# State-space stage: skip products issued behind the exponential, the gated tile's high part in its own step, and the second tile's taps behind the gated tile

## Chip, cores and metric

The kernel runs on 1 core of one Trainium2 chip. The metric is the device time of one execution in microseconds (us), as the median of several executions. All activation and weight tensors are float32; products that must be exact to float32 are split into high and low parts of type fp32r, so that one product becomes three matmuls (high by high, high by low, low by high).

## The reference, cut to what matters

Four layers, each added to a residual after a layer norm: a selective state-space layer (Mamba-2 form), a ternary feed-forward layer, a causal attention and a mixture of 8 experts. The change lies in the first. For 2 sequences of 512 tokens, 64 heads of 64 channels in 8 groups, and a state of 128:

```
proj = hidden @ in_proj_w.T                # gate, x|B|C, dt
xBC  = silu(conv_bias + sum_k shift(hbc, k) * conv_weight[:, k])   # 4 taps
state = state * exp(dt*A) + dt*x (outer) B ;  y = state . C + D*x
var  = mean over the 512 channels of a group of y*y
yn   = y * rsqrt(var + eps) * norm_weight * silu(gate)
out  = yn @ out_proj_w.T
x    = x + layernorm(out)
```

## The kernel before, in words

The state-space stage works group by group (g = 0 to 7, 512 channels each: 4 tiles of 128 channels for x, one for B, one for C). Within a group it goes through steps s = 0 to 7, one for each piece of 128 tokens (4 pieces make one sequence; c is the piece's number in its sequence). `group_steps` writes the steps out for group 0, in a hardware loop for groups 1 to 6, and for group 7, which has two more steps (8 and 9) to drain. Each engine has its own `step` function; the order of the lines in it is the order in which that engine works, and semaphores tie the engines together. A step holds work on three token pieces at once, s, s-1 and s-2:

- TensorE (PE): transposes of piece s (L1604, L1608) and its B.C product (L1610), the decay exponents of piece s (L1618, called D here, into banks 2 and 3), the convolution input of a first new tile (L355 with wch and wcl, 12 passes, bank 0), the column sum of squares of piece s-2 (L1635), then for piece s-1 the product with the entering state (L1644, into bank 6, for c > 0), the products within the piece (L1650, into bank 7) and the state's addition (L1659, into bank 6, for c < 3), the convolution input of a second tile (L355, bank 2), a tile of the gate (L355 with wgh and wgl, bank 0), and last the output product of piece s-2 (L355 with ynTh, ynTl, woh and wol, 12 passes, bank 1).
- Steps 0, 1, 2, 4, 5, 6 have two convolution tiles each; steps 3 and 7 have none, nor have steps 3 to 9 of the last group. D writes bank 2, so it waits until VectorE has applied the taps to the second tile of the step before (`taps`).
- ScalarE (ACT): the copy of the transposed piece s to `xtok` (L965), the high part `ynTh` of piece s-2 (L969), the exponential of piece s in banks 2 and 3 (L974), the first tap and the tanh of each convolution tile (L927, L935), the sum's scaling `ssv` (L986), the square of y of piece s-1 (L993), the gate's tanh (L941), and last the four skip products `xd` = D*x of piece s (L1002). Besides: casts of the next group's weights, in step 2 (L955, woh), step 3 (L979, wch) and step 5 (L1014, wgh, ahead of the exponential), and the scaling of the next output weights at the end of step 7 (L1020).
- VectorE (DVE): copies and mask of piece s (L1291, L1294), the low part `ynTl` of piece s-2 (L360), the masked decays `em` of piece s (L1304), the entering part y (L1278), taps of the first tile (L1200, three instructions), y of piece s-1 (L1316, L1319, which needs `xd`), the state (L1325 or L1328), silu of the first tile (L1206), taps of the second tile (L1200), the gated tile yn of piece s-1 written to bank 6 (L1340), the gate's product (L1253), silu of the second tile (L1206), and the addition of the output of piece s-2 to `acc` (L1351). In the last group each addition is followed by a round of the next layer norm on the piece (`norm_round`: L612, L617, L623, L628, L633, L636).
- GpSimd (POOL): the two halves of the squares' sum (L726, L728), the decays `am` of piece s+1 (L710), low parts of weights (L360: wol in step 2, wcl in steps 3 and 4, wgl in step 5), the state's decay (L746), `dtx` and `xdec` of piece s (L756, L761) and the reciprocal root `rg` (L767).
- SyncE (SP) loads the next group's weights as their buffers come free and the decay factors of each piece (`grown_load`). The diff does not touch it.

Bank 6 holds in turn the product with the entering state, the state's addition and yn. PE's L1644 and L1650 in a step wait for `ynT_lo` of piece s-2, which says that bank 6 has been read; the output product waits for it too. `ynTh` may be overwritten only when the output product of the piece before is done (`o_ready`).

## Time and profile before

| what | us |
|---|---|
| median of 3 runs | 1781.15 |
| the 3 runs | 1765.92, 1786.74, 1781.15 |
| the profiled execution, its own time | 1772.24 |
| its span from first to last instruction | 1770.5 |
| state-space stage, groups 0 to 7 | from about 98 to 1048 |
| one group of the loop | about 117 |

The times in rows are us from the start of the span, durations in rows of groups "mean ns of one". Idle time stands in brackets with what ended it. PE is TensorE's matmuls, PEld its weight loads, which overlap them. A run of matmuls shows the first one's start and the last one's end.

### The profile page before, as it was taken

To read this page: it belongs to the slowest core of one execution; us is meant where nothing else is said; L and a number is where in the kernel's file an instruction comes from. 1 tells how busy PE (TensorE), PEld (TensorE's weight loads), DVE (VectorE), ACT (ScalarE), POOL (GpSimd) and SP (SyncE) were. 2 spreads that over 40 slices of the span, in tenths; PEclk is the share of its full clock that TensorE was granted. 3 is DMA by queue.
4 is the path that set the end of the run, shared out by engine and by line. 5 is a ranking of instruction groups with operands and counts; after the bars stand their busy time and mean duration, and the time that the engine had idled before them with its cause. 6 is when DMAs were issued, how large, how long until landed. Compare 5 with 4: busy or idle time off the path is not lost.

```text
span 1770.5 us, 26605 instructions
## 1 busy us (share of the span) xinstructions
PE 1561.6 (88%) x8870; PEld 1227.9 (69%) x8870; DVE 1221.4 (69%) x2024; ACT 827.5 (47%) x1639; POOL 942.9 (53%) x861
## 2 busy tenths in 40 slices
PE   3789999999999999999999759996789999987791
PEld 2567877877878778778787647885557776766581
DVE  5467778777787777787787665556657767768525
ACT  2355554554554545555554323332147666764131
POOL 3257667577576675775766744004544423328444
PEclk9899999999999999999999878998889999998796
DMA  3102111012021110110211012222000000041335
GB/s 115 36 4 81 34 46 61 16 47 62 14 86 27 47 54 17 47 62 12 77 39 43 18 60 72 71 78 77 0 1 13 13 1 1 1 167 72 119 132 166
DMA packets 49497, 92.60 MB, mean 52 GB/s; under 512 B 8016, under 2 KB 32720, under 8 KB 44176
## 3 DMA queue, kind: packets, MB, share of 16 engines
q1 hardware_dynamic: 45744, 79.58, 14.1%
q0 software_dynamic: 3680, 12.06, 2.1%
q8 instruction: 43, 0.70, 0.2%
q14 instruction: 30, 0.25, 0.0%
HBM read 81.14 MB, written 10.49 MB: 52 GB/s over the span
## 4 chain that ended last, share of the span: by engine, by line
PE 61%; DVE 16%; POOL 8%; issue 7%; ACT 4%; DMA 3%; SPq 1%; POOLq 0%; ACTq 0%; DVEq 0%
PE banks L355 31%; PE banks L1726 6%; PE banks L1852 3%; PE banks L1650 3%; PE banks L1644 3%; PE banks L1736 3%; PE banks L1817 2%; POOL wol L360 2%; DMA x<-in_w_gate 2%; DVE tap L1200 2%; PE banks L1842 2%; PE banks L1659 2%; PE banks L1618 2%; DVE acc L623 2%; DVE xbc L1206 1%
## 5 line engine op out<-in xcount | busy, mean ns | idle before, releaser
L1200 DVE SCALAR_TENSOR_TENSOR tap<-banks,parg,tap 128x511 f32<-128x511 f32 (+2 forms) x288 | 215.0, 747 | 41.4 <-ACT tap L927 33.9
L710 POOL TENSOR_TENSOR am<-ah,upto 128x1024 fp32r<-128x1024 f32 x64 | 126.4, 1975 | 214.0 <-PE banks L1618 198.9
L862 POOL TENSOR_SCALAR kz<-kst,head 128x512 fp32r<-128x512 f32 x64 | 99.1, 1568 | 159.9 <-DVE kst L1427 159.9
L355 PE MATMUL banks<-xTh,wch 128*128 128x512 f32 x384 | 163.4, 425 | 7.0 <-DVE em L1304 6.8
L355 PE MATMUL banks<-xTh,wcl 128*128 128x512 f32 x384 | 151.3, 394 | 0.0
L355 PE MATMUL banks<-xTl,wch 128*128 128x512 f32 x384 | 151.1, 394 | 0.0
L1132 ACT ACTIVATE prob<-banks,nmax 128x128 f32<-128x128 f32 (+3 forms) x256 | 121.8, 530 | 54.5 <-DVE nmax L1438 54.4
L935 ACT ACTIVATE th<-tap 128x512 f32<-128x512 f32 x96 | 60.4, 630 | 171.4 <-DVE tap L1200 169.2
L1438 DVE TENSOR_REDUCE nmax<-banks 128x2 f32<-128x256 f32 (+3 forms) x128 | 104.7, 818 | 40.3 <-PE banks L1843 40.2
L710 POOL TENSOR_TENSOR am<-al,upto 128x1024 fp32r<-128x1024 f32 x64 | 121.9, 1904 | 0.0
L927 ACT ACTIVATE tap<-banks,parg 128x512 f32<-128x512 f32 x96 | 74.5, 776 | 91.4 <-PE banks L355 90.4
L355 PE MATMUL banks<-xTh,wgh 128*128 128x512 f32 x256 | 107.9, 421 | 5.2 <-POOL wgl L360 4.7
L1304 DVE TENSOR_TENSOR em<-banks,gmask 128x1024 f32<-128x1024 f32 x64 | 78.2, 1222 | 43.1 <-ACT banks L974 42.7
L355 PE MATMUL banks<-woh,ynTh 128*128 128x512 f32 x256 | 103.5, 404 | 4.0 <-DVE ynTl L360 4.0
L1852 PE MATMUL banks<-ident,prob 128*128 128x128 f32 x640 | 95.6, 276 | 10.7 <-DVE pB L1448 7.2
L355 PE MATMUL banks<-xTh,wgl 128*128 128x512 f32 x256 | 101.7, 397 | 0.0
L355 PE MATMUL banks<-woh,ynTl 128*128 128x512 f32 x256 | 101.3, 396 | 0.0
L355 PE MATMUL banks<-xTl,wgh 128*128 128x512 f32 x256 | 101.1, 395 | 0.0
L355 PE MATMUL banks<-wol,ynTh 128*128 128x512 f32 x256 | 100.7, 393 | 0.0
L355 PEld LDWEIGHTS banks<-xTh,wch 128*128 128x128 f32 x384 | 72.8, 190 | 36.7 <-DVE em L1304 13.4
L1726 PE MATMUL banks<-xTh,gu 128*128 128x512 f32 x224 | 90.1, 402 | 2.8 <-ACT gu L1059 2.8
L1206 DVE SCALAR_TENSOR_TENSOR xbc<-th,tap 128x512 f32<-128x512 f32 x96 | 90.9, 947 | 0.8 <-ACT th L935 0.8
(289 smaller groups left out, 4396.7 us busy)
## 6 DMA issues: line engine op xcount, KB each, us to landing
x<-grownT SPq DMA_DIRECT2D x96, 128.0 KB, 4.7
x<-in_w_conv SPq DMA_DIRECT2D x7, 1536.0 KB, 6.5
x<-in_w_gate SPq DMA_DIRECT2D x8, 1024.0 KB, 5.0
x<-in_w_out SPq DMA_DIRECT2D x8, 1024.0 KB, 4.8
eraw<-in_expert_w SPq DMA_DIRECT2D x8, 1024.0 KB, 7.2
gur<-in_ff_gu SPq DMA_DIRECT2D x7, 1024.0 KB, 4.8
x<-in_hidden SPq DMA_DIRECT2D x16, 256.0 KB, 3.8
mates<-yd SPq DMA_DIRECT2D x8, 512.0 KB, 4.4
```

The source lines that it names most:

```text
L355: m = nc.tensor.matmul(o, a, b, start=first and n == 0, stop=last and n == len(terms) - 1)
L710: m = pool.tensor_tensor(am[:, part, :, :], a[:, i, :].bitcast(F32).unsqueeze(2).to_broadcast([P, HG, P]), upto[:, :].unsqueeze(1).to_broa ...
L862: m = pool.tensor_scalar(kz[:, quad % 2, p2, j, :], kst[:, p2, :].bitcast(F32), head[:, j:j + 1], None, ALU.mult)
L927: nc.scalar.activation(tap[:, q % 2, :], bk(CONV_BANKS[q % 2]), ACT.Identity, bias=parg[:, CT * KC + q:CT * KC + q + 1], scale=parg[:, KC ...
L935: nc.scalar.activation(th[:, :], tap[:, q % 2, :], ACT.Tanh).then_inc(tanh_ready, 1)
L1132: e = nc.scalar.activation(prob[:, n % 2, j, 0:kw], bk(2 * (n % 2) + j)[:, 0:kw], ACT.Exp, bias=nmax[:, n % 2, j:j + 1])
L1200: nc.vector.scalar_tensor_tensor(tap[:, q % 2, sh:L], bk(CONV_BANKS[q % 2])[:, 0:L - sh], parg[:, KC * q + k:KC * q + k + 1], tap[:, q % 2 ...
L1206: nc.vector.scalar_tensor_tensor(xbc[:, q, b * L:(b + 1) * L], th[:, :], 1.0, tap[:, q % 2, :], ALU.add, ALU.mult).then_inc(xbc_ready, 1)
L1304: nc.vector.tensor_tensor(em[:, s % 2, :, :], decayed, gmask[:, :].unsqueeze(1).to_broadcast([P, HG, P]), ALU.mult).then_inc(m_ready, 1)
L1438: nc.vector.tensor_reduce(nmax[:, n % 2, :], banks[:, 2 * (n % 2):2 * (n % 2) + 2, 0:kw], AX, ALU.max, negate=True).then_inc(max_ready, 1)
L1726: m = mat(bk(2 * w + ft), gu[:, k, ft, w, :], part[:, k, tok], start=(k == 0 and part is xTh), stop=(k == KT - 1 and part is xTl))
L1852: m = pe.transpose(bk(4 + j)[:, c * P:(c + 1) * P], prob[:, w % 2, j, c * P:(c + 1) * P], ident[:, :])
```

## The change

On ScalarE, `ynTh` is no longer made for piece s-2 near the head of step s but for piece s-1 as the last item of step s (ahead of the output weights' scaling in step 7); and the skip products are made for piece s-1 in step s, behind the exponential (and behind the weight casts of step 3), instead of for piece s at the end of step s. On VectorE, yn of piece s-1 is made directly behind the state, ahead of silu of the first tile and of the second tile's taps; `ynTl` of piece s-1 is made at the end of step s, ahead of the addition to `acc`, instead of `ynTl` of piece s-2 near the head; and the copy of the skip factors in step 0 goes to the end of that step, with a second count of `cur_ready` that ScalarE waits for in step 1. No instruction is added or taken away but that count; PE and SP keep their order, and GpSimd's differs by one semaphore value.

```diff
@@ pool, step
                 if s == 0:
-                    pool.wait_ge(cur_ready, g + 1)
+                    pool.wait_ge(cur_ready, 2 * g + 1)
@@ act, step
                     nc.scalar.copy(xtok[:, s % 2, :], bk(4)).then_inc(x_out, 1)
-                if not (first and s < 2):
-                    act.wait_ge(yn_ready, NT * g + i + 1)
-                    at_least(act, o_ready, NT * g + i)
-                    nc.scalar.copy(ynTh[:, :, :], kt(bk(6))).then_inc(ynT_hi, 1)
                 if s == 5 and not last:
                     gate_high(g + 1)
...
                         nc.scalar.copy(couple(wch, n), couple(conv_stage(1), n)).then_inc(wc_hi, 1)
+                if not (first and s == 0) and s <= NT:
+                    at_least(act, y_ready, NT * g + s - 1)
+                    if s == 1:
+                        act.wait_ge(cur_ready, 2 * g + 2)
+                    j = (s - 1) % NT
+                    for k in range(KT):
+                        n = nc.scalar.activation(xd[:, k, :], xbc[:, k, j * P:(j + 1) * P], ACT.Copy, scale=skipg[:, k:k + 1])
+                    n.then_inc(xd_ready, 1)
                 if tiles:
                     first_tap(n0 + tiles[0], tiles[0] % CT)
...
                 if tiles:
                     tanh(n0 + tiles[1], tiles[1] % CT)
-                if s < NT:
-                    if not (first and s == 0):
-                        act.wait_ge(y_ready, NT * g + s)
-                    for k in range(KT):
-                        n = nc.scalar.activation(xd[:, k, :], xbc[:, k, s * P:(s + 1) * P], ACT.Copy, scale=skipg[:, k:k + 1])
-                    n.then_inc(xd_ready, 1)
+                if not (first and s == 0) and s <= NT:
+                    act.wait_ge(yn_ready, NT * g + s)
+                    at_least(act, o_ready, NT * g + s - 1)
+                    nc.scalar.copy(ynTh[:, :, :], kt(bk(6))).then_inc(ynT_hi, 1)
@@ dve, step
-                if not (first and s < 2):
-
-                    dve.wait_ge(ynT_hi, NT * g + s - 1)
-                    low(nc.vector, ynTl[:, :, :], kt(bk(6)), ynTh[:, :, :]).then_inc(ynT_lo, 1)
...
-                if s == 0:
-                    nc.vector.tensor_copy(skipg[:, :], skip[:, bass.ds(g, 1), :].rearrange("p g k -> p (g k)"))
...
+                if making:
+                    dve.wait_ge(gate_used, NT * g + 4 + KT * (i // CH) if i >= 0 else NT * g)
+                    if c < CH - 1:
+                        dve.wait_ge(state_ready, m + c + 1)
+                    dve.wait_ge(sq_ready, NT * g + i + 1)
+                    nc.vector.tensor_tensor(kt(bk(6)), kt(bk(7)), gate_at(i % NT), ALU.mult).then_inc(yn_ready, 1)
                 if s == 3 and not last:
                     dve.wait_ge(wc_hi, 3 * g + KT + 1)
                     low(nc.vector, couple(wcl, 0), couple(conv_stage(1), 0), couple(wch, 0)).then_inc(wc_lo2, 1)
                 if tiles:
                     silu(n0 + tiles[0], tiles[0] % CT, tiles[0] // CT % NB)
                     convolve(n0 + tiles[1], tiles[1] % CT)
-                if making:
-                    dve.wait_ge(gate_used, NT * g + 4 + KT * (i // CH) if i >= 0 else NT * g)
-                    if c < CH - 1:
-                        dve.wait_ge(state_ready, m + c + 1)
-                    dve.wait_ge(sq_ready, NT * g + i + 1)
-                    nc.vector.tensor_tensor(kt(bk(6)), kt(bk(7)), gate_at(i % NT), ALU.mult).then_inc(yn_ready, 1)
                 if gate:
...
                 if tiles:
                     silu(n0 + tiles[1], tiles[1] % CT, tiles[1] // CT % NB)
+                if s == 0:
+                    nc.vector.tensor_copy(skipg[:, :], skip[:, bass.ds(g, 1), :].rearrange("p g k -> p (g k)")).then_inc(cur_ready, 1)
+                if making:
+
+                    dve.wait_ge(ynT_hi, NT * g + i + 1)
+                    low(nc.vector, ynTl[:, :, :], kt(bk(6)), ynTh[:, :, :]).then_inc(ynT_lo, 1)
                 i = s - 2
                 if not (first and s < 2):
                     dve.wait_ge(o_ready, NT * g + i + 1)
```

## Rows read from the trace of the kernel before

**Rows 1.** The page: busy time by engine.
```profile
PE 1561.6 (88%) x8870; PEld 1227.9 (69%) x8870; DVE 1221.4 (69%) x2024; ACT 827.5 (47%) x1639; POOL 942.9 (53%) x861
```

**Rows 2.** Windows: one loop group, the last group (busy us by engine, clock, DMA).
```profile
449.00:566.00 117.00, 113.72 (x630) 92.01 (x630) 91.48 (x137) 61.31 (x120) 79.94 (x69) 1.00 0.17 45
917.00:1046.00 129.00, 106.55 (x572) 85.00 (x571) 91.39 (x159) 49.27 (x102) 81.15 (x82) 0.91 0.14 42
```

**Rows 3.** Waits of PE, 98 to 1046: total us, times, longest.
```profile
PE banks L1644 <- DVE ynTl L360: 21.9, 20, 3.3
PE banks L1635 <- ACT xtok L965: 8.5, 8, 1.2
...
PE banks L355 <- DVE ynTl L360: 4.0, 1, 4.0
PE banks L1650 <- DVE ynTl L360: 3.6, 1, 3.6
```

**Rows 4.** Waits of PE in one loop group, 449 to 566.
```profile
PE banks L1644 <- DVE ynTl L360: 1.5, 2, 0.9
PE banks L1635 <- ACT xtok L965: 1.2, 1, 1.2
```

**Rows 5.** Timeline of PE, step 3 of that group: start, us, what, idle before.
```profile
492.12 1.20 PE L1618 MATMUL banks<-am,after 128*128 128x512 f32 x4
494.51 0.35 PE L1635 MATMUL banks<-ones,y 128*128 128x1 f32 x2 [1.19 <-ACT xtok L965]
...
495.80 1.16 PE L1644 MATMUL banks<-xbc,state 128*128 128x128 f32 x8 [0.93 <-DVE ynTl L360]
```

**Rows 6.** Timeline of ACT, end of step 2 and head of step 3.
```profile
492.63 1.26 ACT L1002 ACTIVATE xd<-xbc,skipg 128x128 f32<-128x128 f32 x4
493.80 0.56 ACT L965 COPY xtok<-banks 128x512 f32<-128x512 f32 x1
```

**Rows 7.** Timeline of DVE, steps 2 and 3 of that group.
```profile
487.28 0.69 DVE L1328 TENSOR_TENSOR state<-banks,state 128x512 f32<-128x512 f32 x1 [1.65 <-POOL state L746]
487.89 1.95 DVE L1206 SCALAR_TENSOR_TENSOR xbc<-th,tap 128x512 f32<-128x512 f32 x1
489.76 2.31 DVE L1200 SCALAR_TENSOR_TENSOR tap<-banks,parg,tap 128x511 f32<-128x511 f32 x3
...
495.06 0.68 DVE L360 TENSOR_TENSOR ynTl<-banks,ynTh 128x512 fp32r<-128x512 f32 x1
```

**Rows 8.** Instructions that touch th: ns min/median/max of the silu, over 96.
```profile
L1206 DVE SCALAR_TENSOR_TENSOR xbc<-th,tap x96: 679/684/4346, 60.7 to 965.5; 128x512 f32<-128x512 f32 x96
```

**Rows 9.** Timeline of DVE, step 0 (456) and step 5 (532): the second tile's taps.
```profile
456.37 2.31 DVE L1200 SCALAR_TENSOR_TENSOR tap<-banks,parg,tap 128x511 f32<-128x511 f32 x3
...
532.36 2.31 DVE L1200 SCALAR_TENSOR_TENSOR tap<-banks,parg,tap 128x511 f32<-128x511 f32 x3
```

**Rows 10.** Timeline of PE: D of steps 1 and 6, which wait for those taps.
```profile
461.26 1.18 PE L1618 MATMUL banks<-am,after 128*128 128x512 f32 x4
...
535.91 1.18 PE L1618 MATMUL banks<-am,after 128*128 128x512 f32 x4
```

**Rows 11.** Timeline of ACT, step 0: the square that the gated tile waits for.
```profile
455.96 0.59 ACT L993 ACTIVATE y<-banks 128x512 f32<-128x512 f32 x1
```

**Rows 12.** Window of 3.4 us behind step 3's waits, another group (clock third from last).
```profile
613.80:617.20 3.40, 3.40 (x19) 2.15 (x17) 3.13 (x4) 1.89 (x4) 3.19 (x5) 0.50 0.06 14
```

**Rows 13.** Timeline of DVE, last group, steps 8 and 9.
```profile
1027.27 0.75 DVE L1351 SCALAR_TENSOR_TENSOR acc<-banks,rg,acc 128x512 f32<-128x512 f32 x1 [0.21 <-PE banks L355]
...
1030.57 0.68 DVE L360 TENSOR_TENSOR ynTl<-banks,ynTh 128x512 fp32r<-128x512 f32 x1
...
1047.87 0.75 DVE L1351 SCALAR_TENSOR_TENSOR acc<-banks,rg,acc 128x512 f32<-128x512 f32 x1 [4.77 <-PE banks L355]
```

**Rows 14.** Timeline of PE, the same stretch.
```profile
1031.31 2.08 PE L1644 MATMUL banks<-xbc,state 128*128 128x128 f32 x8 [2.21 <-DVE ynTl L360]
...
1043.25 0.47 PE L355 MATMUL banks<-woh,ynTh 128*128 128x512 f32 x1 [4.05 <-DVE ynTl L360]
```

## The prediction

> **What bounds the kernel now.** I read the page's busy times first, then windows of one group each, then PE's waits in the stage that the diff touches, and last the timelines of the steps where those waits lie. PE is busy for 1561.6 of 1770.5 us and no other engine passes 69% [rows 1]. The reader is to see that this is an average: in a loop group PE works 113.72 of 117 us at full clock, in the last group 106.55 of 129 us at a mean clock of 0.91 [rows 2]. So a loop group offers 3.3 us of idle PE, seven such groups some 23 us; the last group offers over 20 us and a clock. Whatever the change does on ScalarE and VectorE counts only where PE waits for them.
>
> PE's waits name the change's subject: for `ynTl` it waits 21.9 us before L1644, 4.0 us before the last output product and 3.6 us before one L1650, 29.5 us together; for `xtok` 8.5 us in 8 places [rows 3]. One loop group has 1.5 us of the first (steps 3 and 7) and 1.2 us of the second (step 3) [rows 4]. Seven groups make 10.6 us for `ynTl`; the other 18.9 us lie in the last group, where no convolution stands between D and L1644 and the layer norm's instructions stand ahead of `ynTl` on DVE.
>
> **Step 3 of a loop group.** Before: D runs 492.12 to 493.32, then PE waits 1.19 us for `xtok` and 0.93 us for `ynTl` [rows 5]. `xtok` is late because the four skip products (1.26 us) stand ahead of it on ACT [rows 6]. After: `ynTh` of piece 1 takes their place, a copy of the same size as `xtok` (0.56 us). ACT is free for it at 492.63, the output product before it ended before 492, so `xtok` ends at 492.63 + 0.56 + 0.56 = 493.75 instead of 494.36, 0.6 us earlier. On DVE the second tile's taps end at 489.76 + 2.31 = 492.07 [rows 7]; then come the gate's product, silu and now `ynTl` at once, 3 x 0.68: done at 494.1 instead of 495.74. L1644 then starts at 494.2 instead of 495.80: 1.6 us. The copies and the mask now follow `ynTl` and the addition, so the entering part y starts about 495.5; before, it started 0.1 us behind L1644's end. Of the 1.6 us I therefore take 1.4 us. Bounds: 0.3 us, if those taps come later (below) and hold D; 2.1 us, both waits gone.
>
> The skip products of step 3 now stand behind the exponential and three casts (some 4 us) on ACT. They are needed at L1319, which DVE reached 5 us behind the exponential's start; by that they arrive level with it, between 0.5 us early and 0.7 us late. DVE then only reaches the next group's low part later, and PE is in the gate and output products by then (24 passes, 5.5 us), so I take 0; uncovered it would cost 0.7 us.
>
> **Step 7.** PE waits 0.6 us for `ynTl` (1.5 less 0.9 [rows 4]). `xtok` of step 7 gets `ynTh` ahead of it, which waits for the output product just ended: 0.2 us later; and y follows the mask instead of `ynTl`. I take 0.2 us, between 0 and 0.6. The scaling of the output weights (four instructions, some 2.6 us) now waits behind `ynTh`, which waits for the end of PE's step 7, so `xtok` of the next step 0 comes 1.6 us later; a convolution tile (12 passes, 2.8 us) lies on PE between D and the sum that needs it: 0 with 0.6 us to spare.
>
> **Steps 0, 1, 2, 4, 5, 6: what the order on DVE costs.** The gated tile needs the square, and ACT does that behind the second tile's first tap. Silu of the first tile and the second tile's taps used to fill that wait; now they stand behind it. Step 0: the square ends at 455.96 + 0.59 = 456.55 [rows 11]; then yn 0.69, silu 0.68 and taps 2.31 end at 460.3 instead of 456.37 + 2.31 = 458.68 [rows 9]. D starts at 461.26 [rows 10]: 0.9 us to spare, cost 0. Steps 1, 4 and 6 have the same order and nearly the same distance. In step 2 the state is ready only at 487.97, and silu takes 1.95 us where its usual time is 0.684 [rows 7, 8]: it sits there until POOL's `xdec` is over. yn fits into that time (0.69 of the 1.27 us lost), so the taps end where they did, level with D: 0. But in step 2 the casts of woh and the skip products now push ACT's first tap by 1.4 us, and DVE's taps and y by 0.4: 0.2 us lost before L1659. In step 5 the exponential is late (weight casts ahead of it), the skip products delay the first tap by 1.26 us [rows 6], and yn and silu come behind it: taps end about 2 us later than 532.36 + 2.31 = 534.67 [rows 9], D was at 535.91 [rows 10]: 0.8 us lost, less some 0.5 us because the low part of step 4 no longer meets silu and the gate's weights load that much earlier: 0.3 us. Bounds for all six: a gain of 0.6 us in step 5 alone, or D late by 0.6 us in each, 3.6 us.
>
> The memory page, "SBUF — State Buffer" in the Trainium skill (Who interferes with whom), says that a VectorE instruction with two SBUF inputs and a GpSimd instruction that reads SBUF lock each other out for a whole instruction. Silu is such an instruction, yn (from PSUM) is not, and silu's spread in [rows 8] agrees. By that rule every tile step could lose what silu loses behind the squares' sums on POOL, which start with the same square; by the traces only the instruction's own spread is seen.
>
> One loop group: 1.4 + 0.2 - 0.2 - 0.3 = 1.1 us; seven: 7.7 us (group 0 has the same steps).
>
> **The clock.** Behind step 3's two waits some groups show PE at half clock: 613.8 to 617.2 at 0.50 [rows 12], which costs 1.7 us. Three of seven groups have such a stretch near step 3, though not each group with the waits. With the waits down from 2.1 to about 0.6 us I take half of 5.1 us back: 2.5, between 0 and 5.1.
>
> **Last group.** Steps 8 and 9 first. Before, from one addition to the second next it takes 1047.87 - 1027.27 = 20.6 us [rows 13]: addition, norm, `ynTl` at 1030.57, L1644 at 1031.31 behind a 2.21 us wait and at half clock, output product, addition, norm, `ynTl`, and a last output product behind 4.05 us [rows 14]. After: `ynTl` follows the output product by `ynTh` and itself (0.2 + 0.6 + 0.1 + 0.7 = 1.6 us), so step 8's wait of 2.21 goes, and in step 9 the output product needs neither the addition's norm nor anything else but the addition itself: 4.05 becomes 1.6 to 2. That is 2.2 + 2.2; half clock on L1644 and L1650 (about 2 us) and on the last product (1.7 us) may go with the idle time; I take 5.5 of the 8. Steps 3 to 7 wait 1.97, 1.48, 3.6, 3.33 and 1.75 us for `ynTl` (together 18.4 with the two above, of 18.9). There DVE is the next in line: its work of one step with norm adds up to 9.7 to 11 us beside 9 us of PE, and `ynTl` now waits 0.9 us for `ynTh`. Of 12.1 us I take 8.5. Sum 14; bounds 6 (DVE keeps the pace in steps 3 to 7) and 20.
>
> **The sum.** 7.7 + 2.5 + 14 = 24 us against the profiled execution: 1772.24 - 24 = 1748. That execution stands 8.9 us under the median of the runs shown, 1781.15, so the median becomes 1757 us.
>
> **The rivals.**
> (a) Only the last group gains: in loop groups the late taps in tile steps eat what step 3 gives. For it: DVE has 91.48 busy us of 117 and the slack before D is 0.9 us only. Time: 1781 - 14 = 1767, within 1%.
> (b) More comes: both waits of step 3, the wait of step 5 (0.6) and the clock all go: 7 x 2.4 + 5 + 17 = 39 us, 1742. For it: the gate's weights come earlier; against it: three bounds at their best.
> (c) Slower. One mechanism: silu of the first tile, now behind the square, starts together with POOL's squares' sums or `xdec` and is held; taps and so D of the next step come late in each tile step. 6 x 8 = 48 steps, fewer three in the last group. Slack 0.9 us; it starts to cost where silu takes over 1.6 us, and a silu of 2.6 us in all 45 costs 45 x 1.0 = 45 us against 24 won: 1781 + 21 = 1802. The kernel turns slower when the mean silu passes about 2.1 us. Against it: its median is 0.684, mean some 0.94; the sums on POOL take about 0.7 and 0.5 us, so one of them can hold it by no more than that.
> (d) Nothing moves: another signal (the y entering, ready only after the mask) stands right behind `ynTl` everywhere. Time 1778. Against: 4 us alone at the very end wait for nothing else.
>
> **Chances.** Forecast 0.50, (a) 0.26, (b) 0.15, (c) 0.05, (d) 0.04. A change of 1% (17.8 us) is about what a measurement of this kernel can tell from none. Faster by over that: the forecast but for a tenth of it, (b), and a part of (a): 0.68. Within: 0.27. Slower: 0.05. Range from 1738 to 1777: (b)'s time at the low end, (a) and the border of (d) at the high one.
>
> **What would show it.** Right: PE's wait for `ynTl` falls from 29.5 to under 8 us, for `xtok` from 8.5 to 4 to 6; the last group is shorter by 10 us or more; a loop group takes 115.5 to 116.5 us. Wrong: a new wait of PE at L1618 for taps of L1200 above 10 us in total (rival c or a), silu's mean above 1.5 us, or a wait of L1659 for the entering y in the last group as long as the one removed.

## The result, and the profile after

The changed kernel takes 1735.19 us (median of 4 runs, 1733.55 to 1737.61), the kernel before 1783.95 (4 runs, 1765.92 to 1787.4): ratio 0.9752, 95% interval 0.9714 to 0.9791. It is faster, by 48.8 us between the medians, where 24 were forecast; the time lies 2.8 us below the low end of the range. How large the gain is depends on where it is measured: on another chip, further below, the kernel before took 1766.36 us and the changed one 1736.14, 30.2 us less.

The profiled executions tell where it went. Before it was 1772.24, after 1735.23: 37.0 us.

| stretch of the profiled execution, us | before | after | gain | forecast |
|---|---|---|---|---|
| up to the first transposes of group 0 | 94.75 | 92.2 | 2.5 | none |
| groups 0 to 6, transposes to transposes | 822.92 | 805.49 | 17.4 | 10.2 |
| last group, to the last addition to `acc` | 130.2 | 113.06 | 17.1 | 14 |
| behind it, to the end of the span | 722.6 | 722.75 | -0.1 | none |

The other 11.8 us of the gain between medians are not in these two executions: before's stands 11.7 us under its median, after's stands on its own. First the page after, busy time by engine, then windows of one loop group and of the last group (the columns of [rows 2]):

```profile
PE 1551.4 (89%) x8870; PEld 1216.9 (70%) x8870; DVE 1225.2 (71%) x2024; ACT 827.2 (48%) x1639; POOL 947.4 (55%) x861
```

```profile
445.00:560.00 115.00, 113.84 (x630) 91.50 (x629) 91.78 (x137) 61.20 (x120) 80.32 (x68) 1.00 0.16 46
897.70:1010.70 113.00, 102.56 (x573) 81.15 (x571) 90.19 (x159) 50.37 (x106) 80.96 (x82) 0.95 0.15 47
```

Against [rows 1, 2] the busy times hardly move; idle PE does. A loop group has 1.2 us left of 3.3, the last group 10.4 of 22.5, and its mean clock is 0.95 instead of 0.91. PE's waits, from 92 to 1011 (total us, times, longest):

```profile
PE banks L1637 <- POOL y L728: 6.7, 4, 3.1
PE banks L355 <- DVE em L1302: 4.6, 7, 1.3
PE banks L1637 <- ACT xtok L965: 3.6, 7, 0.5
PE banks L1620 <- DVE tap L1202: 3.0, 4, 1.8
...
PE banks L1661 <- DVE y L1280: 2.1, 3, 1.0
...
PE banks L1646 <- DVE ynTl L360: 0.5, 1, 0.5
```

The 29.5 us for `ynTl` of [rows 3] have become 0.5 (L1644 of before is L1646 here, L1635 is L1637, L1618 is L1620). `xtok` has 3.6 of 8.5, all in step 3; step 7 has no wait. What has come up is small: the squares' sums of POOL, 6.7 us, are the largest, all in the last group.

The sum over the windows of the loop's six groups, before and after:

```profile
sum 707.45, PE 686.28 PEld 554.02 DVE 550.13 ACT 367.69 POOL 478.71; mean PE 114.38 PEld 92.34 DVE 91.69 ACT 61.28 POOL 79.78
```

```profile
sum 692.76, PE 684.19 PEld 549.81 DVE 553.30 ACT 367.66 POOL 482.00; mean PE 114.03 PEld 91.63 DVE 92.22 ACT 61.28 POOL 80.33
```

Six groups take 692.76 instead of 707.45, 14.7 us less. Cut by the first transposes of each step, their steps 0 to 7 come to (us):

| groups 1 to 6 | 0 | 1 | 2 | 3 | 4 | 5 | 6 | 7 |
|---|---|---|---|---|---|---|---|---|
| before | 15.1 | 14.9 | 15.9 | 13.0 (three: 14.5 or 14.6) | 15.1 | 15.8 to 16.0 | 15.9 (one 17.3) | 11.1 or 11.2 |
| after | 15.1 | 14.9 | 15.9 | 11.3 in all | 15.4 | 16.1 to 16.9 | 15.9 or 16.6 | 10.4 |

Step 3 gives 14.9 us over the six groups: 1.7 in each, and 1.6 more in each of the three that had PE at half clock. Step 7 gives 4.5, step 4 takes 2.0 and step 5 takes 2.7 back; step 6 comes out even. Group 0 gives another 2.7. Step 3 of one group, PE, then ACT, DVE and POOL:

```profile
482.36 1.20 PE L1620 MATMUL banks<-am,after 128*128 128x512 f32 x4
484.08 0.35 PE L1637 MATMUL banks<-ones,y 128*128 128x1 f32 x2 [0.52 <-ACT xtok L965]
484.36 1.16 PE L1646 MATMUL banks<-xbc,state 128*128 128x128 f32 x8
```

```profile
482.88 0.57 ACT L1005 CAST ynTh<-banks 128x512 fp32r<-128x512 f32 x1
483.35 0.59 ACT L965 COPY xtok<-banks 128x512 f32<-128x512 f32 x1
```

```profile
483.01 0.69 DVE L1208 SCALAR_TENSOR_TENSOR xbc<-th,tap 128x512 f32<-128x512 f32 x1
483.62 0.68 DVE L360 TENSOR_TENSOR ynTl<-banks,ynTh 128x512 fp32r<-128x512 f32 x1
```

```profile
483.65 1.90 POOL L710 TENSOR_TENSOR am<-ah,upto 128x1024 fp32r<-128x1024 f32 x1 [1.91 <-PE banks L1620]
```

From D's start to L1644's place PE needs 484.36 - 482.36 = 2.0 us; before it was 495.80 - 492.12 = 3.68 [rows 5]. `ynTl` ends at 484.30, 0.06 us before it would be waited for. And silu starts 0.64 us ahead of POOL's `am`, which matters below. Over all 96 silus after, ns min, median, max:

```profile
L1208 DVE SCALAR_TENSOR_TENSOR xbc<-th,tap x96: 681/693/2239, 59.0 to 944.9; 128x512 f32<-128x512 f32 x96
```

The largest of [rows 8], 4346 ns, is gone.

### The profile page after: what moved, and what is told of

It is laid out like the page before. It is cut to its first block, busy times and chain, and to the rows that moved or that the text cites. A ratio compares the mean times of both kernels' runs of the same rounds, so it can differ in the third digit from the quotient of the medians.

```text
span 1733.5 us, 26612 instructions
## 1 busy us (share of the span) xinstructions
PE 1551.4 (89%) x8870; PEld 1216.9 (70%) x8870; DVE 1225.2 (71%) x2024; ACT 827.2 (48%) x1639; POOL 947.4 (55%) x861
## 3 DMA queue, kind: packets, MB, share of 16 engines
q1 hardware_dynamic: 45744, 79.58, 14.4%
## 4 chain that ended last, share of the span: by engine, by line
PE 60%; DVE 15%; POOL 8%; issue 7%; ACT 5%; DMA 3%; SPq 1%; POOLq 0%; ACTq 0%; DVEq 0%
PE banks L355 29%; PE banks L1728 6%; DVE tap L1202 3%; PE banks L1854 3%; PE banks L1738 3%; PE banks L1819 2%; PE banks L1620 2%; PE banks L1652 2%; PE banks L1646 2%; DMA x<-in_w_gate 2%; PE banks L1844 2%; POOL wol L360 2%; PE banks L1661 2%; DVE acc L623 1%; DVE nmax L1440 1%
## 5 line engine op out<-in xcount | busy, mean ns | idle before, releaser
L710 POOL TENSOR_TENSOR am<-ah,upto 128x1024 fp32r<-128x1024 f32 x64 | 121.9, 1905 | 187.4 <-PE banks L1620 138.2
L360 POOL TENSOR_TENSOR awl<-prob,awh 128x512 fp32r<-128x512 f32 x8 | 10.1, 1297 | 145.2 <-ACT awh L1090 132.9
```

The lines of the kernel that those rows point to most:

```text
L710: m = pool.tensor_tensor(am[:, part, :, :], a[:, i, :].bitcast(F32).unsqueeze(2).to_broadcast([P, HG, P]), upto[:, :].unsqueeze(1).to_broa ...
```

## The experiments

### Is it the step, or the start and the clock? Before once more

The same code as the kernel before, no edit; ten executions.

> The kernel before, unchanged, for a second profile and the clock of each run. Theory (half clock varies): PE's half-clock stretches behind step 3's two waits come in a changing number of loop groups, so executions differ by 1.7 us per group hit and the times spread over 10 to 20 us; this profile shows step 3 at 13.0 or 14.6 us, and a number of hit groups other than three would explain times above the 1772 us profiled. Rival (start-up): the spread lies ahead of the groups, in the first loads (94.75 against 92.2 us at the first step); then step 3 is hit in three groups again.

Measured: 1775.03 us (1771.21 to 1788.75), ratio 0.9997 [0.9973, 1.0022] to before on that chip. Its first step starts at 93.82, with no change in the code; over all profiles of this study, whatever the version, that start lies between 91.6 and 94.8, so the 2.5 us at the start can't be put down to the change. Groups 0 to 6 take 824.91, but other groups are slow now: step 3 of groups 1 to 6 takes 11.9, 13.0, 17.4, 13.0, 16.2 and 14.6 us. So half clock does vary, as the theory said, but 11.9, 16.2 and 17.4 are times that it did not have. The reason stands in these lines. In before's profiled execution, DVE and POOL in step 3:

```profile
493.40 0.68 DVE L1206 SCALAR_TENSOR_TENSOR xbc<-th,tap 128x512 f32<-128x512 f32 x1
```

```profile
493.40 2.44 POOL L710 TENSOR_TENSOR am<-ah,upto 128x1024 fp32r<-128x1024 f32 x1 [1.91 <-PE banks L1618]
```

In the same code run again, POOL, DVE, then PE behind them:

```profile
490.17 1.90 POOL L710 TENSOR_TENSOR am<-ah,upto 128x1024 fp32r<-128x1024 f32 x1 [1.88 <-PE banks L1618]
```

```profile
490.19 2.42 DVE L1206 SCALAR_TENSOR_TENSOR xbc<-th,tap 128x512 f32<-128x512 f32 x1
```

```profile
494.32 2.07 PE L1644 MATMUL banks<-xbc,state 128*128 128x128 f32 x8 [2.67 <-DVE ynTl L360]
```

The last silu of step 2 (on DVE behind step 3's start) and `am` start within 0.02 us of each other, and one of them gets through first. If it is silu, `am` takes 2.44 us instead of 1.90 and nobody waits. If it is `am`, silu takes 2.42 instead of 0.68, and `ynTl` and L1644 come 1.7 us late. This second outcome is called a lost tie below. The recorded starts do not tell the outcomes apart: in group 2 of the same execution silu is recorded at 373.07 and `am` at 373.06, and silu got through first. With the lost tie PE here ran at half clock. The window behind it:

```profile
493.90:500.70 6.80, 6.38 (x29) 4.71 (x30) 3.88 (x6) 2.26 (x4) 3.75 (x5) 0.54 0.07 13
```

Such a group costs 3.2 to 4.4 us more (16.2 and 17.4 against 13.0). The tie was lost in none of the loop's six groups in the first execution and in two of them in this one. Estimated from these two, six lost ties would be 19 to 26 us, the size of the 21 us between before's own executions. How often it was lost in those that were not profiled can't be seen. The Trainium skill's page "SBUF — State Buffer" (Who interferes with whom) has the mechanism: two-input VectorE instructions and GpSimd reads shut each other out, and "Issue order, not op shape, decides who blocks." The trace agrees, with 2.42 against 0.68 us and 2.44 against 1.90.

### The tie broken alone

```diff
 # before, POOL, ahead of am
+                    if s == 3:
+                        pool.wait_ge(xbc_ready, conv_made(g, s, last))
```

> The kernel before with one wait added: in step 3 GpSimd starts am only when silu of step 2's second tile is done. Theory (silu and am start within 0.1 us of each other in step 3; where am wins, silu takes 2.42 us, ynTl and L1644 come 1.7 us later and PE falls to half clock): no silu of 2.4 us in steps 2 and 3 is left, step 3 never exceeds 14.6 us in a loop group, and the fast executions come closer together; the time is 0.993 to 1.0 of before, since am itself starts 0.6 us later. Rival (half clock comes from the 2.1 us of waits whatever the collision): step 3 spreads as before, with stretches over 15 us.

Measured: 1770.92 (1761.2 to 1775.41, ten executions), ratio 0.9945 [0.9923, 0.9966]. POOL's `am` in one group, with silu now started 1.1 us earlier (368.73), and then the first silu of step 5 in another:

```profile
369.82 1.90 POOL L710 TENSOR_TENSOR am<-ah,upto 128x1024 fp32r<-128x1024 f32 x1 [1.99 <-PE banks L1620]
```

```profile
521.65 4.35 DVE L1208 SCALAR_TENSOR_TENSOR xbc<-th,tap 128x512 f32<-128x512 f32 x1
```

No loop group has half clock, and no tie is lost. Step 3 takes 13.0 us in group 1, where the first silu of step 2 takes 1.94 us beside POOL's `xdec` as it does in before, and 11.9 in the other five, where it takes 0.91. That is a second tie: there silu starts 0.3 us ahead of `xdec` while POOL's `dtx` runs, and it gets in between the two or not, with the same starts. It got in between in none of the six groups of before, in one of before again, and in five of the skip-only kernel below, which has no wait added. Each time it is worth 1.0 us of step 3, and silu then is a microsecond ahead of `am` anyway. A third is the first silu of step 5 beside POOL: in four groups it takes 4.35 us and the step behind it 17.3 instead of 15.9, in before this happens in one group (the 4346 ns of [rows 8]).

Groups 1 to 6 take 701.7 us against 707.45; the last group stays at 130.14. These 5.7 us are not the worth of the order of silu and `am`: before had lost no tie in the loop either, and only in group 1 could the added wait change their order. They are the second tie's outcome, half clock gone, and three more long silus of step 5. What the added wait is worth is seen between medians alone, some 8 us, with an interval from 6 to 14. This is in line with lost ties in the executions that were not profiled, but no profile shows them. The executions still spread by 14 us, as other places part too.

### Each part alone

```diff
 # high part only, in act and dve; before's places are taken out
+                if not (first and s == 0) and s <= NT:
+                    act.wait_ge(yn_ready, NT * g + s)
+                    at_least(act, o_ready, NT * g + s - 1)
+                    nc.scalar.copy(ynTh[:, :, :], kt(bk(6))).then_inc(ynT_hi, 1)
...
+                if making:
+                    dve.wait_ge(ynT_hi, NT * g + i + 1)
+                    low(nc.vector, ynTl[:, :, :], kt(bk(6)), ynTh[:, :, :]).then_inc(ynT_lo, 1)
 # skip products only: the block with at_least(act, y_ready, ...) and xd of the change, skipg's copy last in step 0
 # gated tile only, in dve: the gated tile's block ahead of
                 if tiles:
                     silu(n0 + tiles[0], tiles[0] % CT, tiles[0] // CT % NB)
                     convolve(n0 + tiles[1], tiles[1] % CT)
```

> The kernel before with only ynTh at the end of its own step and ynTl ahead of the addition; skip products stay at the step's end (now ahead of ynTh), the gated tile stays behind the second tile's taps. Theory (the last group pays by this part alone, the loop groups need the skip products out of ACT's way): last group shorter by 13 to 17 us, loop groups within 0.7 us of the 116.8 before, since ACT has skip products, ynTh and xtok in a row before step 3's sum (a wait of about 1.7 us for xtok); time 0.983 to 0.992 of before. Rival (this part does it all): loop groups at 115 to 115.5 us and a ratio of 0.975 to 0.98.

> The kernel before with only the skip products behind the exponential. Theory (each part alone leaves the next signal a few tenths of a us behind, so the parts pay together): xtok no longer keeps PE waiting in step 3 (8.5 to under 3 us), but ynTl behind the mask does, for longer than the 21.9 us before; time 0.995 to 1.003. Rival (additive): 0.987, what the changed kernel lost when this part alone was undone.

> The kernel before with only the gated tile ahead of silu and the second tile's taps. Theory (its worth is that silu of the second tile follows its taps 0.7 us sooner and starts ahead of am): no silu of 2.4 us at the start of step 3, step 3 steady at 12 to 13 us in all loop groups, time 0.993 to 0.999; the last group unchanged within 2 us. Rival (additive): 0.987.

| kernel | median | ratio [95%] | groups 1 to 6 | last group |
|---|---|---|---|---|
| before | | | 707.45 | 130.2 |
| high part only | 1758.49 | 0.9879 [0.983, 0.9929] | 712.96 | 118.65 |
| skip products only | 1774.84 | 0.9965 [0.9939, 0.9992] | 708.5 | 132.52 |
| gated tile only | 1766.59 | 0.9919 [0.9887, 0.9951] | 708.57 | 130.91 |
| the change | 1735.19 | 0.9752 [0.9714, 0.9791] | 692.76 | 113.06 |

(One of the ten executions with the skip products only took 5288.1 us; it is not in the median.) In the profiled executions no part alone shortens the loop; the last group is the high part's alone, 11.6 us here where 13 to 17 were expected. The high part makes the loop 5.5 us longer, against an expectation of 0.7 us a group: one tie is lost, and in five of the six groups the first silu of step 5 takes 4.3 us. What the others leave behind is in the waits of PE. Skip products only:

```profile
PE banks L1646 <- DVE ynTl L360: 30.9, 21, 5.6
```

The wait for `xtok` is gone, and PE waits for `ynTl` instead, as the theory had it. Gated tile only, silu of the whole run, then PE's waits:

```profile
L1206 DVE SCALAR_TENSOR_TENSOR xbc<-th,tap x96: 679/693/2565, 59.1 to 964.8; 128x512 f32<-128x512 f32 x96
```

```profile
PE banks L1635 <- ACT xtok L965: 6.4, 16, 0.8
PE banks L1618 <- DVE tap L1200: 5.9, 8, 1.6
```

The last silu of step 2 does not meet `am` (in group 3 it starts at 492.41, `am` at 493.71), no loop group has half clock, and each takes 118.07 to 118.11 us. It is level, not short: step 3 takes 12.1 us, but steps 2 and 6 take 16.6 and 16.8 instead of 15.9, and step 7 takes 11.8 instead of 11.2. The executions run from 1765.43 to 1772.65, the profiled one being the slowest, and their median is 12.5 us under before's, a little more than was expected. That this is won back where before loses ties is an inference: the profiled loop is 1.1 us longer than before's.

### Two parts of three

```diff
 # changed, without the skip products' move (act; skipg's copy and cur_ready as in before)
+                if s < NT:
+                    if not (first and s == 0):
+                        act.wait_ge(y_ready, NT * g + s)
...
+                    n.then_inc(xd_ready, 1)
                 if not (first and s == 0) and s <= NT:
                     act.wait_ge(yn_ready, NT * g + s)
 # changed, without the gated tile's move (dve): its block stands ahead of
                 if gate:
                     if making:
```

> The changed kernel with its skip products put back to the end of step s, ahead of ynTh. Theory: step 3 loses what the change won there, 1.3 us or more for xtok in each loop group, so 8 to 15 us slower than the changed kernel, a ratio of 0.98 to 0.99 to before. Rival (place of skip products doesn't matter, since ACT has idle time): within 3 us of the changed kernel.

> The changed kernel with the gated tile put back behind the second tile's taps. Theory (that order costs or gives nothing in loop groups, by the 0.9 us of slack before D): within 3 us of the changed kernel, and steps 4 and 5, which grew by 0.35 us each, back at 15.1 and 15.9 us. Rival (the early gated tile is what lets ynTh and the low part follow at once): 5 us or more slower, with step 7 back at 11.1 us.

Without the skip products' move: 1753.63 (1750.31 to 1757.76), 0.9871 [0.9837, 0.9904]; groups 1 to 6 take 707.4, last group 117.76. PE's waits, and step 3 on ACT and PE:

```profile
PE banks L1635 <- ACT xtok L965: 14.0, 16, 1.2
```

```profile
493.07 1.27 ACT L998 ACTIVATE xd<-xbc,skipg 128x128 f32<-128x128 f32 x4
...
494.70 0.58 ACT L965 COPY xtok<-banks 128x512 f32<-128x512 f32 x1
```

Skip products and `ynTh` both stand ahead of `xtok`, which is late in steps 3 and 7 of every group: 11.6 or 11.7 and 11.3 us instead of 11.3 and 10.4. These two steps make 7.7 of the 14.7 us by which groups 1 to 6 trail the change; the other half is in steps 2 and 6, at 16.6 and mostly 16.8 us as in the gated-only kernel. So the medians are 18 us apart where 8 to 15 were expected, and the wait for `xtok` is only half of it. Without the gated tile's move: 1752.89 (1747.87 to 1757.76), 0.987 [0.983, 0.991]; 707.19 and 113.78. This was expected within 3 us of the changed kernel and is 17 us slower, and the rival's sign, step 7 back at 11.1 us, fails as well (10.4). Here three of six groups lose the tie, as in these lines of DVE, POOL and PE:

```profile
488.43 2.42 DVE L1208 SCALAR_TENSOR_TENSOR xbc<-th,tap 128x512 f32<-128x512 f32 x1
```

```profile
488.41 1.90 POOL L710 TENSOR_TENSOR am<-ah,upto 128x1024 fp32r<-128x1024 f32 x1 [1.89 <-PE banks L1620]
```

```profile
491.51 1.16 PE L1646 MATMUL banks<-xbc,state 128*128 128x128 f32 x8 [2.21 <-DVE ynTl L360]
```

Its groups without the lost tie take 116.2 us, those with it 119.3 to 119.7. So of the 14.4 us by which it trails the change in groups 1 to 6, some 10 are three lost ties; the other 4 are mostly step 3 at 11.9 instead of 11.3.

In the profiled loops the parts don't add up, because they work on the same step. In step 3 L1644 is held by the later of `xtok` and `ynTl`. The skip products' move frees ACT for `xtok`; the high part's move frees `ynTl`. With yn ahead of the taps, yn fills the time in which the first silu of step 2 waited beside `xdec` (silu takes 1.95 us in [rows 7], 1.15 after), and no longer stands between the two silus; so the second one starts 0.64 us ahead of `am`, in every loop group of both profiled executions of the changed kernel. No profile with the gated tile's move has a lost tie. The medians are less clear: the three parts alone gave 19.4, 4.3 and 12.5 us against before on their chips, 36 together, and all three gave 30.2 to 48.8 by the chip. They neither show nor exclude that the parts add up. The third pair, skip products and gated tile without the high part, was not run.

### The last group

```diff
 # before, but ynTh and ynTl at their new places in the last group only
-                if not (first and s < 2):
+                if not (first and s < 2) and not (last and s > 0):
...
+                if last and s <= NT:
...
+                if making and last:
```

> The kernel before with ynTh and ynTl in their own step in the last group only, nothing else. Theory: the last group shortens from 130 to 118 or 119 us (as in the run with this part in all groups) and groups 0 to 6 stay within 4 us of before: a ratio of 0.992 to 0.995. Rival (the last group's gain needs the earlier groups' order or the skip products' place): the last group stays above 124 us.

Measured: 1764.63 (1753.98 to 1768.96), 0.9917 [0.9887, 0.9948]; the profiled execution is the fastest. Last group 113.88 us, groups 0 to 6 822.83, as before. So 16.3 of the 17.1 us are this one move, more than was expected of it. The same move in all groups gave 118.65 above; that execution had half clock for 20.4 us of the last group, this one for 10.2, and 10.2 us more at half speed are at most 5.1 us of work, about the difference of 4.8. Part of the gain is of this kind too: the last group of before had half clock for 23.8 us, the changed kernel's for 10.2, so up to 6.8 of the 17.1 us are PE's speed and not its waits. The wait that stands next, of PE:

```profile
PE banks L1643 <- POOL y L728: 8.4, 4, 3.2
```

In the changed kernel, DVE and then PE in steps 8 and 9:

```profile
997.09 0.74 DVE L1353 SCALAR_TENSOR_TENSOR acc<-banks,rg,acc 128x512 f32<-128x512 f32 x1
...
1004.69 0.69 DVE L360 TENSOR_TENSOR ynTl<-banks,ynTh 128x512 fp32r<-128x512 f32 x1 [0.65 <-ACT ynTh L1005]
...
1010.75 0.75 DVE L1353 SCALAR_TENSOR_TENSOR acc<-banks,rg,acc 128x512 f32<-128x512 f32 x1 [2.08 <-PE banks L355]
```

```profile
997.23 1.16 PE L1646 MATMUL banks<-xbc,state 128*128 128x128 f32 x8 [0.49 <-DVE ynTl L360]
...
1004.62 0.38 PE L1637 MATMUL banks<-ones,y 128*128 128x1 f32 x2 [2.26 <-POOL y L728]
1006.09 0.50 PE L355 MATMUL banks<-woh,ynTh 128*128 128x512 f32 x1 [1.08 <-DVE acc L1353]
```

The two steps that took 20.6 us [rows 13] take 1010.75 - 997.09 = 13.66. PE's last output product waits 1.08 us for the addition where it waited 4.05 for `ynTl` [rows 14].

### Can the rest be had?

The changed kernel again, beside two variants on the same chip: `ynTh` at the head of the next step but behind `xtok`, with the wait for step 4's parameters behind both; and POOL's squares' sums of piece s-1 ahead of its norm work in the last group.

```diff
 # high part at the next head (act), the change's place taken out
                     nc.scalar.copy(xtok[:, s % 2, :], bk(4)).then_inc(x_out, 1)
+                if not (first and s < 2):
+                    act.wait_ge(yn_ready, NT * g + i + 1)
+                    at_least(act, o_ready, NT * g + i)
+                    nc.scalar.copy(ynTh[:, :, :], kt(bk(6))).then_inc(ynT_hi, 1)
 # squares first (pool)
+                if not (first and s < 2) and not (last and s > 3):
+                    squares(NT * g + s - 1)
...
+                if last and 3 <= s <= NT:
+                    squares(NT * g + s)
```

> The changed kernel, unchanged, on the chip of the next two runs. Theory (silu of step 2's second tile starts 0.6 us ahead of am and can't lose to it): every loop group has step 3 at 11.3 us again, the executions lie within 5 us of each other where those of the kernel before spread over 15, ratio 0.973 to 0.978. Rival (the steady step 3 of the first profile was luck): some group shows a silu of 2.4 us there and a step 3 over 13 us.

> The changed kernel with ynTh put back behind xtok at the head of the next step (the wait for the step-4 parameters moved behind it), while ynTl stays at the end of its step on VectorE. Theory (what pays is that ynTl no longer stands behind addition, norm and mask; ynTh's own place is worth only the transposes it no longer waits for): loop groups within 1 us of the changed kernel's 115 to 115.8; in the last group each step with VectorE as its limit grows by up to 1 us, since xtok waits for the transposes: 116 to 120 us instead of 113; in all 3 to 10 us slower than the changed kernel. Rival (the place of ynTh is the change): the last group back above 125 us.

> The changed kernel with GpSimd's two squares' sums ahead of the norm's instructions in steps 3 to 8 of the last group, instead of at the head of the next step. Theory (PE's largest new wait, 6.7 us for those sums, comes from the norm's roots and additions ahead of them on GpSimd): the waits fall under 2 us, the last group shortens by 3 to 6 us, time 2 to 6 us under the changed kernel. Rival (VectorE is the limit of those steps, the sums are not): last group within 1 us of 113.

| kernel | median (range) | ratio [95%] | last group |
|---|---|---|---|
| before, there | 1766.36 (1764.38 to 1770.7) | | |
| changed again | 1736.14 (1734.37 to 1737.23) | 0.9823 [0.9806, 0.984] | 113.27 |
| high part at the next head | 1747.45 (1745.31 to 1748.96) | 0.9887 [0.9869, 0.9905] | 118.25 |
| squares first | 1740.43 (1740.15 to 1743.85) | 0.9846 [0.983, 0.9862] | 118.0 |

Step 3 is 11.3 us in every loop group again, and the changed kernel is within 1 us of what it was. Before is 1766 on this chip and 1779 on another, and its seven executions lie within 6.3 us here, so the ratio is 0.9823, outside the 0.973 to 0.978 expected. `ynTh` at the next head loses 11.3 us (the profiles differ by 11.1, of which 1.2 lie ahead of the first step), a little over the 3 to 10 expected, with the loop and the last group as its theory had them. So the place of `ynTh` is worth 3.9 us in groups 1 to 6 and 5.0 in the last group. PE's waits there are

```profile
PE banks L1646 <- DVE ynTl L360: 10.7, 18, 1.3
PE banks L1661 <- DVE y L1280: 9.3, 11, 3.1
```

Squares first loses 4.3 us, against the theory that the 6.7 us of waits for them could be had; the rival's last group within 1 us of 113 fails too. PE's wait only changes its name, and DVE's norm work shows why, here and then in the changed kernel:

```profile
PE banks L1664 <- DVE y L1283: 9.7, 4, 5.5
```

```profile
980.82 2.01 DVE L623 TENSOR_SCALAR acc<-acc,mv,rs 128x512 f32<-128x512 f32 x1
...
982.75 2.11 DVE L628 TENSOR_SCALAR acc<-x,mv,rs 128x512 f32<-128x512 f32 x1
```

```profile
976.75 0.59 DVE L623 TENSOR_SCALAR acc<-acc,mv,rs 128x512 f32<-128x512 f32 x1
977.26 2.12 DVE L628 TENSOR_SCALAR acc<-x,mv,rs 128x512 f32<-128x512 f32 x1
```

POOL's `am` now lies beside both and not only the second, and they hold y of the next piece. Half clock adds to it, 13.6 us in this last group and 6.8 in the changed kernel's run again. A last try put the round of the norm behind `em` of the next step, so that y does not stand behind it:

```diff
 # dve, behind em
+                if last and s >= 3:
+                    norm_round(1, s - 3)
...
-                    if last and i >= 0:
-                        norm_round(1, i)
```

> The changed kernel with the norm's round on a piece, in the last group, moved from the end of a step to the next step behind em, so that the entering part of y (which the state's addition L1661 waits for) no longer stands behind it on VectorE. Theory (with ynTl early, VectorE's work is the limit of steps 5 to 8, so where its norm stands matters only by latency): L1661's wait for y (2.1 us) goes, the last group shortens by 1 to 5 us. Rival (the norm's instructions with only SBUF operands meet am on the shared port there as well, as they did with the squares' sums moved): 2 us or more slower.

Measured: 1735.55 (1735.13 to 1736.66), 0.9768 [0.9722, 0.9815], last group 112.16, 1.1 us less than in the run again. The wait for y is down to 0.4 us, and the squares' sums, 7.9 us there, take it up:

```profile
PE banks L1638 <- POOL y L728: 9.2, 4, 3.1
```

Its time can't be told from the changed kernel's. No version tried here is faster than that.

## Why the prediction was right and wrong

- **The sum over the profiled execution: 24 said, 37.0 measured.** The 13 us are 2.5 at the start (not shown to be the change's), 4.9 in the loop's steps (7.7 said, 12.6 measured), 2.3 of clock in step 3 and 3.1 in the last group.
- **Direction and where PE waits: right.** `ynTl` falls to 0.5 us (under 8 was said), `xtok` to 3.6 (4 to 6 was said), the last group is 17.1 us shorter (10 or more), a loop group takes 115.0 to 115.8 (115.5 to 116.5). D waits 3.0 us for taps, not 10.
- **Step 3: the term held.** 1.4 us was said, 1.7 measured: both waits went but 0.5 us. The kernel without the skip products' move waits 14.0 us for `xtok`, so it is their place that lets it come early; without the high part's move PE goes on waiting for `ynTl`, 27.5 us or more.
- **Step 7: mis-sized, the largest miss of the loop's steps.** 0.2 us was taken, 0.7 to 0.8 measured: the wait for `ynTl` went (0.6), and the 0.4 taken off because "`xtok` of step 7 gets `ynTh` ahead of it" and y follows the mask did not come. The high part alone gives the 10.4 us; of the versions with `ynTh` at its own step's end only the one with the gated tile early and the skip products still ahead of `ynTh` has `xtok` late there (11.3).
- **Steps 2, 4, 5 and 6: nearly right.** Step 2 lost nothing (0.2 was said), steps 4 and 5 lost 0.3 and 0.3 to 1.0 (0 and 0.3), step 6 0.7 in some groups. For step 4 the prediction left out the copy of the next parameters on DVE, which ACT waits for ahead of `xtok`. The copy now comes behind `ynTl` and beside POOL's `am`. Before, then after:

```profile
505.69 0.17 DVE L1184 COPY parg<-par 128x34 f32 x1
```

```profile
495.18 1.67 DVE L1186 COPY parg<-par 128x34 f32 x1
```

  ACT waits 3.2 us for it, where it waited 2.4 before (its waits from 492 to 508.5):

```profile
ACT xtok L965 <- DVE parg L1186: 3.2, 1, 3.2
```

  With the wait behind `xtok` (the next-head variant, where the copy takes 0.80 us) step 4 is back at 15.1 us. Step 6's 0.7 us stand in just those groups where the first silu of step 5 takes 2.03 us instead of 1.0: two of the six in one profile of the changed kernel, four in the other.

- **The clock: the step that failed by its size.** "I take half of 5.1 us back: 2.5" was said; all of it came back, 4.8 us in the three steps 3. In steps 1 to 7 of group 0 and in the loop, neither profiled execution of the changed kernel has a stretch at half clock; nor has the gated-only kernel, the one without the skip products' move, or the one with the tie broken alone. Before has four, in groups 0, 2, 4 and 5. Beside or behind each of the seven lost ties in the profiles of this study (two in before again, three without the gated tile's move, one each in the high-part-only and the last-group kernel) stands a stretch at half clock. But before has it with the tie won, the skip-only kernel too, and the gated-only kernel keeps full clock with two waits of PE in each step 3. Why some groups with the same waits have it and others not stays open.
- **The median: the step that failed by its mechanism.** "That execution stands 8.9 us under the median of the runs shown, so the median becomes 1757 us" carried before's distance over as a constant. It isn't one. After the change the profiled execution stands on its median, and the whole distance, 11.7 us by then, became gain. Ties and half clock differ from execution to execution of before. The change takes the tie with `am`, the one with `xdec` and half clock out of the loop, and leaves one silu of step 5 that costs 0.7 us or not: its executions lie within 4 us, before's within 21. That the ties make the distance is shown for single groups, and the 8 us of the kernel with the tie broken point to it; for the whole of it, it is not shown. It also depends on the chip: where before's median was 1766.36, under the profiled 1772.24, the gain was 30.2 us, nearer to the forecast. By the profiled executions alone the comparison is 1748 against 1735, by the medians 1757 against 1735. The lock-out of silu, which rival (c) took for a danger of the change, was at work against before. [Rows 8] had a trace of it in the maximum of 4346 ns, in step 5 of one group; the tie with `am` could not be seen there, as it was won in every group of the loop. It shows only by start times: silu at 493.40, `am` at 493.40.
- **The last group: mis-sized by 3 us.** "Sum 14" was said, 17.1 measured, of it 16.3 by the high part alone. Steps 8 and 9 together gave 6.9 of the 8 where 5.5 were taken; the other 10.2 lie in steps 3 to 7, where 8.5 were taken because DVE was thought to be the next in line at 9.7 to 11 us a step. Steps 5 and 6 there take 7.0 and 13.8 after 12.0 and 14.3 before, steps 3 and 4 12.0 and 9.6 after 15.5 and 11.2: DVE does not keep the pace down as was feared. Its norm work no longer stands ahead of `ynTl`.
- **The rivals.** (a) fell: the loop gained 17.4 us. (b), more comes, was nearest with 1742, but by luck as much as by its mechanism: of its conditions only the clock was met in full. Step 3 keeps 0.5 us of its waits, step 5 keeps 0.5 of its 0.6, and a group gave 1.8 us without the clock, not 2.4; what made up for it was the median's distance. (c) fell: silu's median is 0.693 us, D's wait 3.0 us. (d) fell with the first.

## What to carry to other kernels

Before costing an order change, put the start times of two-input VectorE instructions and GpSimd's beside each other over all repeats of the loop: where they fall within some hundredths of a microsecond, or where both stand behind the same earlier GpSimd instruction, the profiled execution shows one outcome of several, and a change that sets the order for good is worth the mean of what the tie costs, not what this execution paid. A large spread of a kernel's own executions is a sign to look for it, and the distance of one execution from the median is not to be added to a forecast as a constant. Look also at what a moved instruction's neighbours will run beside: a copy of 0.17 us took 1.67 here. And when several signals meet at one wait, forecast the set of edits: here neither a part alone nor the two pairs tried shortened the profiled loop by more than 0.3 us, and all three gave 14.7 us.

## What the runs showed of the hardware that was not expected

- A tie within 0.02 us goes one way or the other between executions of the same code, and between groups of one execution: silu at 0.68 or 2.42 us, `am` at 2.44 or 1.90. Another does so with 0.3 us between the starts: silu at 0.91 or 1.95 us, `xdec` at 1.50 or 1.05.
- The level of before differed by the chip it ran on: its median is 1766.36, 1776.57, 1777.93 and 1779.1 on four chips, the changed kernel's 1735.19 and 1736.14 in its two runs. Whether the ties are the reason is not shown.
- Single-input copies and scalings on VectorE suffer beside GpSimd too. The copy of the decay factors, ns min, median and max over the groups, in before and then in the changed kernel:

```profile
L1288 DVE COPY cur<-per x8: 249/250/253, 95.1 to 918.5; 128x192 f32 x6, 128x192 f32<-128x192 f32 x2
```

```profile
L1290 DVE COPY cur<-per x8: 253/1819/1822, 92.6 to 899.8; 128x192 f32 x6, 128x192 f32<-128x192 f32 x2
```

  The same copy costs seven times as much where it falls beside GpSimd's `am`. The Trainium skill's page "SBUF — State Buffer" (Who interferes with whom) names copies and scalings as operations that can take the port pair shared with GpSimd, under conditions that no run here tests; these rows agree.
- Where half clock starts differs: with 2.67 us of waiting PE fell to half clock within the wait, and L1644 took 2.07 us; with 2.21 us of waiting in another kernel the same product took 1.16, and the clock fell 1.4 us behind its start.
